# Head attention with scores and exponentials in two halves of two PSUM banks

## The reference

```python
scores = jnp.einsum('bhqd,bhkd->bhqk', q, k) / jnp.sqrt(jnp.float32(hd))
attn = jax.nn.softmax(scores, axis=-1)
attn = jnp.einsum('bhqk,bhkd->bhqd', attn, v)
...
dots = jnp.where(causal, mask_value, dots)      # in two of the three
```

## Time and profile before

| | us |
|---|---|
| median of 3 runs | 7849.85 |
| lowest, highest | 7842.77, 7853.74 |
| the profiled execution's own time | 7852.84 |
| its span in the profile | 7851.0 |
| the three attention calls together (298 + 301 + 318) | about 917 |

### The profile page before, as it was taken

The page is one execution under the profiler, slowest core; times in us unless marked ns, Lnnn a source line. Parts: engine busy times, 40 slices in busy tenths (PEclk is TensorE's granted clock), DMA queues, the critical chain, the costliest instruction groups (busy, mean ns, idle before and its releaser), DMA issues. The chain is left out here.

```text
span 7851.0 us, 113325 instructions
## 1 busy us (share of the span) xinstructions
PE 6900.6 (88%) x35879; PEld 3837.7 (49%) x35879; DVE 4362.2 (56%) x5633; ACT 2980.3 (38%) x4668; POOL 2192.6 (28%) x1465
## 2 busy tenths in 40 slices
PE   6868878788788899899989899989979899899998
PEld 2422222223223466466634466556634477566676
DVE  4549999999996455455434455455544311354111
ACT  4543333333333333333344333333334333433333
POOL 1206656566563122122202122122212100000000
PEclk8979999999999899999989899999989899988899
DMA  0000000000000000000000000000000000000000
GB/s 34 0 0 0 0 0 0 0 0 0 0 0 20 2 0 0 0 0 0 0 1 0 2 0 0 0 0 0 0 22 1 5 0 0 0 0 0 1 0 11
DMA packets 1684, 19.82 MB, mean 3 GB/s; under 512 B 176, under 2 KB 176, under 8 KB 688
## 3 DMA queue, kind: packets, MB, share of 16 engines
q1 hardware_dynamic: 1584, 18.47, 0.6%
HBM read 16.37 MB, written 2.10 MB: 2 GB/s over the span
## 5 line engine op out<-in xcount | busy, mean ns | idle before, releaser
L2111 POOL TENSOR_TENSOR wbig<-wbig 128x1024 f32<-128x1024 f32 x512 | 1204.3, 2352 | 663.3 <-DVE wbig L2092 663.3
L2014 PE MATMUL banks<-wbig 128*128 128x512 f32 x2080 | 1041.6, 623 | 338.0 <-POOL wbig L2111 338.0
L2092 DVE TENSOR_TENSOR_SCAN wbig<-banks,wbig 128x1024 f32<-128x1024 f32 x512 | 1172.7, 2290 | 40.0
L2048 ACT ACTIVATE banks<-banks,wbig 128x1020 f32<-128x1020 f32 x512 | 555.6, 1085 | 726.6 <-PE banks L2008 726.6
L2014 PEld LDWEIGHTS banks<-wbig 128*128 128x128 f32 x2080 | 357.4, 191 | 831.8 <-POOL wbig L2111 548.2
L1475 POOL TENSOR_TENSOR arena<-arena,wbig 128x512 f32<-128x512 f32 x256 | 325.5, 1272 | 1457.4 <-DVE arena L1388 1456.8
L601 DVE TENSOR_REDUCE arena<-banks 128x4 f32<-128x1024 f32 (+1 forms) x384 | 401.6, 1046 | 434.3 <-PE banks L435 306.2
L2087 DVE TENSOR_TENSOR wbig<-banks,arena 128x1024 f32<-128x1024 f32 x512 | 613.7, 1199 | 22.8 <-PE banks L2008 22.8
L1021 DVE SCALAR_TENSOR_TENSOR arena<-banks,arena 128x128 f32<-128x128 f32 x512 | 144.1, 344 | 844.2 <-PE banks L930 844.2
L989 ACT ACTIVATE arena<-banks,wbig 128x512 f32<-128x512 f32 x512 | 351.8, 687 | 537.1 <-PE banks L946 528.0
L2008 PE MATMUL banks<-arena,wbig 96*128 x2048 | 529.0, 379 | 1.1 <-DVE wbig L2087 1.1
(11 more groups left out here) (298 smaller groups left out, 12213.0 us busy)
## 6 DMA issues: line engine op xcount, KB each, us to landing
wbig<-in_l_ffn SPq DMA_DIRECT2D x1, 4185.0 KB, 13.0
wbig<-in_l_ffn SPq DMA_DIRECT2D x1, 3925.5 KB, 12.3
X<-in_x SPq DMA_DIRECT2D x1, 2048.0 KB, 12.5
out_x<-X SPq DMA_DIRECT2D x1, 2048.0 KB, 6.3
wsmall<-in_l_attn_a SPq DMA_DIRECT2D x1, 1573.5 KB, 6.3
wbig<-in_ssm_scan SPq DMA_DIRECT2D x1, 1151.5 KB, 8.3
cst<-in_constants SPq DMA_DIRECT2D x1, 1033.0 KB, 14.6
wsmall<-in_l_attn_b SPq DMA_DIRECT2D x1, 914.5 KB, 4.5
```

The costliest lines, as they stand in the source:

```text
L2014: last = pe.matmul(y_bank[:, h, :], onehot[u], hc[u][:, h * TILE:(h + 1) * TILE], start=False, stop=True, skip_group_check=True)
L2048: act.activation(decay, decay, ACT.Exp, scale=neg_a[:, bass.ds(g * 32 + j * 2 + u, 1)]).then_inc(act_in.sem, 1)
L2092: dve.tensor_tensor_scan(bx[u], decay_bank[u].rearrange("p h c -> p (h c)"), bx[u], 0.0, ALU.mult, ALU.add)\
L2111: pool.tensor_tensor(hc[u], bx[u], cq, ALU.mult).then_inc(pool_in.sem, 1)
```

## The change

A round's scores and exponentials are made in two halves, "a" for the groups 0 and 1 (banks 0 and 1) and "b" for the groups 2 and 3. PE does all matmuls of half a, signals, and then those of half b. ACT makes one exponential for each half, of two banks. Each half has its own steps (`s0a`, `s0b`, `e0a`, ...). Half a of a round waits for half a of the exponentials before it and half b for half b. `values` waits for half b. The two looks of a round stay where they were.

```diff
-    pe_s = Steps(k, "scores", ["s0", "late", "s1", "pv0", "s2", "pv1", "s3", "pv2"], BATCH + 1)
-    act_s = Steps(k, "exponentials", ["e0", "ln", "recip", "e1", "shift1", "e2", "e3"], BATCH + 1)
+    pe_s = Steps(k, "scores", ["s0a", "s0b", "late", "s1a", "s1b", "pv0", "s2a", "s2b", "pv1", "s3a", "s3b", "pv2"],
+                 BATCH + 1)
+    act_s = Steps(k, "exponentials", ["e0a", "e0b", "ln", "recip", "e1a", "e1b", "shift1", "e2a", "e2b", "e3a", "e3b"],
+                  BATCH + 1)
...
                 if s == 0:
                     pe.wait_ge(pool_s.sem, pool_s.at(i, "qm"))
-                    pe.wait_ge(act_s.sem, act_s.before(i, "e3"))
-                else:
-                    pe.wait_ge(act_s.sem, act_s.at(i, f"e{s - 1}"))
-                for g in range(4):
-                    pe.matmul(sbank[:, g, :, first:SEQ], kf[par][rows(g), c * 128:(c + 1) * 128],
-                              qm[par][rows(g), 2 * jj:2 * jj + 2, first:SEQ], start=True, stop=True)
...
+                for part, both in (("a", (0, 1)), ("b", (2, 3))):
+                    pe.wait_ge(act_s.sem, act_s.at(i, f"e{s - 1}{part}") if s else act_s.before(i, f"e3{part}"))
+                    for g in both:
+                        pe.matmul(sbank[:, g, :, first:SEQ], kf[par][rows(g), c * 128:(c + 1) * 128],
+                                  qm[par][rows(g), 2 * jj:2 * jj + 2, first:SEQ], start=True, stop=True)
+                    if s == 0 and part == "a":
+                        pe.wait_ge(act_t.sem, act_t.at(i, "shift0"))
+                    elif s == 2 and part == "a":
+                        pe.wait_ge(act_s.sem, act_s.at(i, "shift1"))
+                    for g in both:
+                        last = pe.matmul(sbank[:, g, :, first:SEQ], k.cb["ones"][rows(g), :],
+                                         shift[rows(g), 2 * jj:2 * jj + 2, first:SEQ], start=False, stop=True,
+                                         skip_group_check=True)
+                    if causal:
+                        for g in both:
+                            last = pe.matmul(sbank[:, g, :, c * 128:(c + 1) * 128], k.cb["ident"],
+                                             twice(k.cb["causal_kq"]), start=False, stop=True, skip_group_check=True)
+                    last.then_inc(pe_s.sem, 1)
...
-                pe.wait_ge(act_s.sem, act_s.at(i, f"e{s}"))
+                pe.wait_ge(act_s.sem, act_s.at(i, f"e{s}b"))
...
-                act.wait_ge(pe_s.sem, pe_s.at(i, f"s{s}"))
...
+                for part, both in (("a", slice(0, 2)), ("b", slice(2, 4))):
+                    act.wait_ge(pe_s.sem, pe_s.at(i, f"s{s}{part}"))
+                    act.activation(prob[s % 2][:, both, :, first:SEQ].rearrange("p g j t -> p (g j) t"),
+                                   sbank[:, both, :, first:SEQ].rearrange("p g j t -> p (g j) t"), ACT.Exp,
+                                   scale=scale).then_inc(act_s.sem, 1)
```

More of the change, by code:

```diff
@@ L473, in scores @@
-                last.then_inc(pe_s.sem, 1)
+                for part, both in (("a", (0, 1)), ("b", (2, 3))):
[16 more added lines that the diff above has]
+                    last.then_inc(pe_s.sem, 1)
@@ L521, in _ @@
             trip(BATCH - 1, 1, False, True)
-            pe_s.skip(pe, BATCH, "s0")
+            pe_s.skip(pe, BATCH, "s0a", "s0b")
             values(BATCH - 1, 1, 3)
-            pe_s.skip(pe, BATCH, "s1", "pv0", "s2", "pv1", "s3", "pv2")
+            pe_s.skip(pe, BATCH, "s1a", "s1b", "pv0", "s2a", "s2b", "pv1", "s3a", "s3b", "pv2")
         @block.scalar
@@ L534, in shifts @@
                     act.wait_ge(pe_m.sem, pe_m.at(b, "turned0"))
-                    act.wait_ge(pe_s.sem, pe_s.before(b, "s1"))
+                    act.wait_ge(pe_s.sem, pe_s.before(b, "s1b"))
                 else:
                     act.wait_ge(pe_t.sem, pe_t.at(b, "turned1"))
-                    act.wait_ge(pe_s.sem, pe_s.before(b, "s3"))
+                    act.wait_ge(pe_s.sem, pe_s.before(b, "s3b"))
                 for j in (2 * jj, 2 * jj + 1):
@@ L545, in exponential @@
                 first = 128 if causal and c else 0
-                act.wait_ge(pe_s.sem, pe_s.at(i, f"s{s}"))
-                act.activation(prob[s % 2][:, :, :, first:SEQ].rearrange("p g j t -> p (g j) t"),
-                               sbank[:, :, :, first:SEQ].rearrange("p g j t -> p (g j) t"), ACT.Exp, scale=scale)\
-                    .then_inc(act_s.sem, 1)
+                for part, both in (("a", slice(0, 2)), ("b", slice(2, 4))):
[3 more added lines that the diff above has]
+                                   scale=scale).then_inc(act_s.sem, 1)
             def reciprocal(b):
@@ L575, in _ @@
             trip(BATCH - 1, False, True)
-            act_s.skip(act, BATCH, "e0")
+            act_s.skip(act, BATCH, "e0a", "e0b")
             reciprocal(BATCH - 1)
-            act_s.skip(act, BATCH, "e1", "shift1", "e2", "e3")
+            act_s.skip(act, BATCH, "e1a", "e1b", "shift1", "e2a", "e2b", "e3a", "e3b")
         @block.vector
```

## The result

| | us |
|---|---|
| before, median of 4 runs | 7846.31 (7838.50 to 7853.74) |
| changed kernel, median of 4 runs | 7968.72 (7952.04 to 7971.35) |
| ratio | 1.0152, 95% interval 1.0134 to 1.0169 |
| forecast | 7962, range 7925 to 7992 |

A forecast was written before the change was run, and what follows sets the result against it. PE, 88 to 96% busy in the three calls, was taken as the bound. Causal 60, causal with bias 46 and without mask 6 us sum to 112, on the median 7849.85 giving 7962 us, range 7925 to 7992.

The forecast's parts named there:

- PE bounds, and an earlier exponential helps no one: All three calls: PE sets the pace, ACT waits for it; gain only 1.7 us in each causal call's last trip.
- The causal rounds: Causal calls: half b runs behind half a, adding 1.39 us to a 512-column round and 0.87 to a 256-column one.
- The covers of rounds 0 and 1: Causal calls: POOL's wait cuts round 0's cost to 0.67 us; with bias, the bias wait hides round 1's 0.87.
- The sum: Whole kernel: 60 us causal, 46 causal with bias and 6 without mask, together 112 us.
- The call without mask: Half b's scores start at 0.96 us, during a's subtraction; +0.12 us in three rounds of 16 trips, 6 us.
- The rule on matmuls in one queue: PE's queue: matmuls stay in program order, only weight loads are pulled ahead, so half b stays behind half a.
- The rival of cheap halves: Half b's passes run beside half a's; about 0.22 us a causal round, some 20 us, 7870 us; chance 5%.
- The fallen clock: Three calls: two working strips might bring 1.2 GHz; each tenth at the lower level adds 77 us, 8040; chance 3%.

The follow-up runs named there:

- e7: e5 plus POOL's product in two halves, and round 0's values waiting for DVE's product instead of its bias; 7759.29 us, ratio 0.9915.
- e8: The same three changes as e7 on the kernel before, scores and exponentials of a round whole; 7763.58 us, ratio 0.9915.
- e1: Changed kernel with the causal calls' mask matmuls moved behind the scores and subtractions of both halves; 7864.95 us, ratio 1.0047.
- e4: Causal calls as in e1; in the call without mask, one 16-column matmul of all 128 rows added to the changed kernel's half a; 7891.02 us, one run.
- e3: Causal calls as in e1; in the call without mask, each group's scores followed at once by its subtraction, in quarters; 7860.02 us, one run.
- e2: Changed kernel with PE as it was, but ACT making one exponential of all four banks after half b; 7966.93 us, ratio 1.0177.
- e5: Changed kernel with the mask matmuls of all four groups ahead of a causal round's scores; 7815.86 us, ratio 0.9982.
- e6: e1 with POOL's product for the looks made in two halves, look 0 waiting for the first alone; 7790.63 us, ratio 0.9955.

## Why the prediction was right

- **PE bounds, and an earlier exponential helps no one.** Right. PE is busy in 324 of 324 us in the causal call, ACT waits 50 us more, and e7 against e8 shows it for the causal calls even with PE's other waits gone.
- **The causal rounds.** +1.39 and +0.87 us were forecast, 3.20 - 1.83 = 1.37 and 2.14 - 1.30 = 0.84 came. Two groups cost as much as four: the second half has the same 0.96 us from scores to subtraction as the first. e1 shows that nothing else is in the loss.
- **The covers of rounds 0 and 1.** Right in the loops of the causal calls: POOL's wait is gone there, and of the waits for the bias 0.3 us are left. A trip in the loop is 3.69 us longer in the causal call (3.80 forecast) and 2.85 in the one with bias (2.93). But the prediction misread: of the 15 waits for POOL one, of 6.3 us, is at the call's start, and only 14 are in trips. The first trip had no such wait to cover its round 0, and the last has no look 0. At full clock four rounds of the first trip would cost 4.4 us; it is 9.8 and 8.8 us longer, and the remaining 5.4 and 4.4 go with the longer time at 1.2 GHz (last section). The last trip is 2.4 and 1.9 us longer (2.1 forecast).
- **The sum.** Part of how near it came is luck. In the calls it is 115 us for 112, but that is 5.5 us less than forecast without mask, 1.5 us less in the loop of the causal call and 1.1 in that with bias, and some 12 us more in the causal calls' first and last trips, of which 10 belong to the clock. (The 60 us of the causal call are 59.1 by the prediction's own terms.)
- **The call without mask.** The sum was near, 0.5 us for 6, but the step was wrong: "half b's scores start at 0.96, while a's subtraction runs". They start 0.22 us after half a's, where groups 2 and 3 had started before. Rows pointed that way: in the earlier trace rows the scores of groups 0 and 1 start together with the odd look that stands ahead of them, and only those of groups 2 and 3, whose strips the look uses, are 0.22 us behind. I took the queue's order for the order of the strips. With it the forecast that POOL's wait before look 0 falls to 0.7 us failed: it stayed at 1.41, and DVE's at 0.25.
- **The rule on matmuls in one queue.** The Trainium skill ("TensorE: Matmul & The Clock Gate", Part 2) says that matmuls stay in program order. For the starts the runs say otherwise on different strips: the look of e4 at 307.66 starts ahead of the second passes at 307.87 that stand before it. The measurement decides. For the signals e4 agrees: DVE got this look's signal only after half b's subtraction. In the causal calls the rule gave the right number only because all-row matmuls stand between the halves.
- **The rival of cheap halves** had the right mechanism for the call without mask, and for the causal calls the wrong end: it let half b run past the mask matmuls. The causal calls show that it can't, and e4 that one of 16 columns is enough.
- **The fallen clock** came in a small form: 13.6 and 10.2 us more at 1.2 GHz at the start of the two causal calls, none later in them.

## What to carry to other kernels

Here matmuls of 32 rows ran beside each other across everything in the queue that was not on their own strips, and one matmul of all rows, of only 16 columns, ended that. So put all-row matmuls together, next to others of their kind, and never between groups of row-tiled ones. And before work is cut in halves so that the next engine can begin sooner, look which engine waits: a signal that is early for an engine with 50% idle time buys nothing, and what the cut costs on the engine that is 96% busy is paid in full.

## What the runs showed of the hardware

**Strips overtake each other.** In e4 a bf16 matmul on strips 0 and 1 started 0.21 us before float32 passes on strips 2 and 3 that were queued ahead of it. Its signal did not overtake them. In the 14 trips of the loop DVE began on each of the three looks that had gone ahead 0.72 to 0.81 us after the look's end, and 0.08 to 0.17 us after that of half b's subtraction; in the changed kernel and in e3, where no look goes ahead, it begins 0.04 to 0.13 us after the look. So a start ahead of the queue's order does not bring the result forward for an engine that waits for its signal. Whether the matmul itself finished late or only its signal was held isn't shown, since the ends of matmuls in the profile are modelled.

**The clock rose later where the halves ran apart.** In both causal calls the granted clock was at the lower level (1.2 GHz) for 34.1 us at the call's start, where it was 20.5 and 23.9 us before and the same in e1, which differs from the changed kernel only in the place of the masks and of the signal of half a. Windows of the changed kernel, then of e1:

```profile
4112.00:4123.00 11.00, 10.64 (x54) 3.78 (x54) 2.61 (x3) 3.05 (x6) 3.02 (x6) 0.50 0.01 2
```

```profile
4111.00:4390.00 279.00, 269.30 (x3569) 135.50 (x3573) 119.62 (x135) 129.94 (x219) 75.36 (x115) 1.00 0.00 1
```

PE is busy in 10.64 of 11 us there, so it wasn't for want of matmuls in flight. 13.6 and 10.2 us more at half speed would be at most 7 and 5 us; the first trips have 5.4 and 4.4 us that full clock doesn't explain. e4 points the same way: the call without mask was at the lower level until 34 us after its first instruction, and until 27 to 29 us in before, the changed kernel, e1, e2, e3 and e8. That two strips at a time are the reason was not tried by itself.

**Blocks with unchanged code move by 10 us.** In the changed kernel, e1, e2, e3 and e8 the first window attention call is 10.5 to 10.8 us longer, in e4, e5, e6 and e7 it is not. At its end, and on into the next blocks, the clock is low for 41 us instead of 14. The same stretch in the kernel before and in e1:

```profile
3190.00:3222.00 32.00, 22.88 (x131) 17.27 (x131) 7.31 (x17) 6.47 (x11) 1.88 (x1) 0.86 0.00 0
```

```profile
3190.00:3222.00 32.00, 28.02 (x117) 21.56 (x116) 3.02 (x12) 3.50 (x8) 0.00 (x0) 0.58 0.00 0
```

The two expert calls have 495.5 us each before, with 27 us at the lower level, and are up to 13.6 us shorter in other kernels (in the changed kernel 483.6 us with 3 us and 488.7 with 14). This belongs to e1's 37 us over before, where the attention calls don't differ: the runs of e1 had a mean granted clock of 0.944 to 0.946, those of before beside them 0.947 to 0.950. As an estimate, 0.005 of the clock in some 7850 us would cost up to 40 us if PE bound all of it, so the clock can account for the 37. But the only trace of before is of an execution of 7852.84 us and none of the 7828 that it took on that chip, so it stays open in which blocks the rest of the 37 us lies, and what decides when the clock falls. A change of 10 or 20 us in this kernel is better read from the lengths of the calls than from the medians.
